# A two-unit loop body with a reordered slot, and transposes as two 64-row halves, in a software-pipelined attention and feed-forward kernel

## The chip, the cores and the metric

The kernel runs on one core of a Trainium2 chip. The core has five engines that run their own instruction streams and meet only in semaphores: TensorE (PE; its weight loads are shown apart as PEld), VectorE (DVE), ScalarE (ACT), GpSimd (POOL) and SyncE (SP, which starts the DMAs). The metric is the device time of one launch in microseconds (us); the kernel before takes 3991.84 us, the median of three runs (3988.70 to 3993.46). The profile is of one further execution, which took 3979.11 us.

## The reference

Batch 32, sequence 128, width 128, float32. First comes one cross-attention layer with residual, then a layer norm, then six layers of local attention and feed-forward, then the second residual. A "unit" below is one batch row in one of the six layers, so there are 6 x 32 = 192 units:

```python
for i in range(DEPTH):                                   # DEPTH = 6
    x = attn_layer(shift_tokens(x), Wqkv[i], q_scale[i], k_scale[i], Wo[i]) + x
    x = ffn_layer(shift_tokens(x), ln_g[i], ln_b[i], W1[i], b1[i], W2[i], b2[i]) + x
# attn_layer: q, k, v = split(x @ Wqkv) into 16 heads of 64
#   q = rotary(l2norm(q) * qs) * scale;  k = rotary(l2norm(k) * ks) / scale
#   softmax over windows of 32 queries and the 64 keys of this and the previous window
#   out = (softmax @ v) @ Wo
# ffn_layer: layer norm, a, gate = split(xn @ W1 + b1);  (a * gelu(gate)) @ W2 + b2
```

`shift_tokens` moves half of the channels by one token.

## The kernel before

After the cross-attention phase the kernel runs "slots". In slot n each engine executes its part of a fixed, hand-written list for several units at once: queries and keys of unit a = n are projected, unit m = n-1 is normalized, unit b = n-2 is transposed, scored and put through the softmax, unit c = n-3 is multiplied with its values, and unit d = n-4 gets output projection and feed-forward. Semaphore counts carry every dependence. Within a slot the engines do this:

- PE: `proj_qk(0)`, two groups of 4 transposes (L1089, queries), the token-shift matmuls of `zm` (L1119, L1120), `proj_qk(1)`, the transposes of the keys (L1089), `proj_qk(2)`, the transpose of the next input (L1134), `scores` (L1144, L1152), the transposes of the softmax P (L1167), the transpose of the normalized row (L1172), `proj_qk(3)`, the two W1 products (L1181, L1185), `proj_v(0)`, `attend` (L1103), `proj_v(1)`, the W2 product (L1201, "y2") and last the Wo product (L1210, "y"). The values of unit b are projected two slots after its queries, so the transposed input `zsT` has four buffers, and the loop body holds four slots.
- ACT copies what PE wrote from the PSUM banks: squares of the projections (L552), queries and keys (L561), P (L605), `zsT`, `znT` (L612); then a table load (L615), the fourth square, gelu (L623), a table load (L626), exp (L630), values (L568) and attention output `oT` (L574).
- DVE: `rotary(j)` (L814, a multiply into `ta` and one into `tb` for each of four banks), nine small operations `root(0)` to `root(8)` (L822 to L841) for 1/norm, the feed-forward residual chain `zm`, mean and variance, `zn` (L851 to L885), row maximum and subtraction (L896, L901), `hT` (L913), the row sums of P (L920), the sums of squares `ss` (L926), the reciprocal (L930) and `z_sb`, the unit's result (L935).
- POOL: `add(j)` (L436) joins `ta` and `tb`, `normalize(j)` (L445) multiplies by 1/norm, L478 multiplies P by the reciprocal; L452, L467 and L472 are small.
- SP copies values with a row offset (`shift_v`) and reloads the weights of the next layer.

The loop over slots is a `Fori` (the profile gives its register and branch instructions the line L244); 45 passes of four slots run in it, the first ten and the last eight slots are written out. The cross-attention phase has a loop of its own (L259 for its branch).

## Time and profile before

| | |
|---|---|
| median of 3 runs | 3991.84 us |
| profiled execution | 3979.11 us, span 3977.3 us |
| PE busy | 3528.5 us, 89%, 60708 matmul instructions and as many weight loads |
| DVE, ACT, POOL busy | 3481.0 us (88%), 2616.5 us (66%), 2522.5 us (63%) |
| mean granted TensorE clock | 0.965 of full |

A float32 product is shown as two matmul instructions with a weight load each, a transpose as one. Busy PE time is not PE at its peak, since matmuls are pipelined. The span splits into the cross-attention phase and start (about 0 to 400 us), the written-out first slots, the loop, and the written-out end (from 3842 us).

### The profile page before, as it was taken

The numbers are of one execution on the slowest core, as the hardware profiler recorded it, in microseconds if no ns is written. First come the engines' busy times: TensorE is split into PE (matmuls) and PEld (weight loads), VectorE is DVE, ScalarE is ACT, GpSimd is POOL, SyncE is SP. The second block draws the span as 40 slices with busy tenths as digits, with TensorE's granted clock in tenths as the row PEclk, the third lists the DMA queues.
The fourth block names the chain that finished last, engine by engine and source line by source line (L and its number), as shares of the span: only waits on it lengthen the run. The fifth ranks groups of instructions, "written<-read, shape, count | busy, mean of one in ns | idle before, by whom it ended". The sixth has DMA issues, their size and how long they took to land.

```text
span 3977.3 us, 158623 instructions
## 1 busy us (share of the span) xinstructions
PE 3528.5 (89%) x60708; PEld 2531.4 (64%) x60708; DVE 3481.0 (88%) x7219; ACT 2616.5 (66%) x4783; POOL 2522.5 (63%) x2671
## 2 busy tenths in 40 slices
PE   6887799998998989989989989989989889899997
PEld 3444476666666666666666666666666666666665
DVE  7888898998898988889989988889889889888895
ACT  3445676776676766667767676666667667666675
POOL 3334576766666766666667666666667667666673
PEclk9878899999999999999999999999999999999998
DMA  2000111112211112211111211112211112211112
GB/s 66 5 5 4 25 49 44 48 44 54 66 42 50 42 49 55 59 50 42 50 42 54 67 42 50 42 42 67 53 47 45 47 45 60 61 42 45 47 44 60
DMA packets 126086, 184.83 MB, mean 46 GB/s; under 512 B 26742, under 2 KB 49332, under 8 KB 124724
## 3 DMA queue, kind: packets, MB, share of 16 engines
q1 hardware_dynamic: 125492, 175.28, 17.2%
q8 instruction: 571, 9.36, 0.9%
q14 instruction: 23, 0.19, 0.0%
HBM read 21.32 MB, written 2.10 MB: 6 GB/s over the span
## 4 chain that ended last, share of the span: by engine, by line
PE 53%; ACT 21%; issue 20%; DVE 4%; ACTq 1%; POOL 0%; DMA 0%; DVEq 0%; SPq 0%; POOLq 0%
PE bank L1066 13%; PE bank L1210 10%; PE bank L1089 9%; PE bank L1152 6%; ACT L615 6%; ACT oT L574 4%; ACT gl L623 4%; PE bank L1167 4%; PE bank L972 2%; ACT znT L612 2%; ACT L626 2%; ACT vt L568 2%; PE bank L1144 2%; PE bank L1013 1%; PE bank L1120 1%
## 5 line engine op out<-in xcount | busy, mean ns | idle before, releaser
L436 POOL TENSOR_TENSOR qk<-ta,tb 128x512 f32<-128x512 f32 x768 | 971.6, 1275 | 513.3 <-DVE tb L814 513.3
L552 ACT ACTIVATE sq<-bank 128x512 f32<-128x512 f32 x768 | 459.3, 598 | 777.9 <-PE bank L1066 771.2
L1066 PE MATMUL bank<-wqkv,zsT 128*128 128x512 f32 x1536 | 831.1, 624 | 114.0 <-issue 104.9
L445 POOL TENSOR_TENSOR qk<-qk,rn 128x512 f32<-128x512 f32 x768 | 776.5, 1042 | 72.9 <-DVE rn L841 72.9
L814 DVE TENSOR_TENSOR ta<-bank,rot 128x512 f32<-128x512 f32 x768 | 529.4, 689 | 259.5 <-ACT sq L552 259.3
L478 POOL TENSOR_TENSOR P<-P,rowsum 128x512 f32<-128x512 f32 x384 | 393.6, 1044 | 498.9 <-DVE rowsum L930 498.9
L814 DVE TENSOR_TENSOR tb<-bank,rot 128x512 f32<-128x512 f32 x768 | 523.0, 681 | 0.0
L1089 PEld LDWEIGHTS bank<-cst,qk 128*128 128x128 f32 x3072 | 376.4, 146 | 214.4 <-issue 213.6
L1210 PE MATMUL bank<-wo,oT 128*128 128x128 f32 x3072 | 393.6, 281 | 130.3 <-ACT oT L574 130.2
L1210 PEld LDWEIGHTS bank<-wo,oT 128*128 128x128 f32 x3072 | 357.4, 191 | 167.1 <-ACT oT L574 128.5
L926 DVE TENSOR_REDUCE ss<-sq 128x32 f32<-128x2048 f32 x192 | 437.0, 2276 | 0.0
L1077 PE MATMUL bank<-wqkv,zsT 128*128 128x512 f32 x768 | 414.6, 622 | 10.8 <-DVE tb L814 4.2
L1089 PE MATMUL bank<-cst,qk 128*128 128x128 f32 x3072 | 415.0, 280 | 0.0
L605 ACT ACTIVATE PT<-bank 128x512 f32<-128x512 f32 x384 | 209.0, 595 | 305.4 <-PE bank L1167 305.4
L1103 PEld LDWEIGHTS bank<-PT,vs 64*64 64x64 f32 x18432 | 286.9, 135 | 145.7 <-issue 145.7
L1152 PE MATMUL bank<-kT,qT 64*32 64x64 f32 x24576 | 291.4, 224 | 41.1 <-issue 40.9
L1066 PEld LDWEIGHTS bank<-wqkv,zsT 128*128 128x128 f32 x1536 | 239.9, 197 | 132.0 <-issue 117.5
L1152 PEld LDWEIGHTS bank<-kT,qT 64*32 64x32 f32 x24576 | 281.3, 105 | 58.4 <-issue 48.1
L920 DVE TENSOR_REDUCE rowsum<-P 128x16 f32<-128x1024 f32 x192 | 234.2, 1220 | 93.1 <-ACT P L630 92.6
L1103 PE MATMUL bank<-PT,vs 64*64 64x32 f32 (+1 forms) x18432 | 308.1, 220 | 0.0
L1181 PEld LDWEIGHTS bank<-znT,w 128*128 128x128 f32 (+1 forms) x1152 | 138.6, 181 | 191.1 <-ACT znT L612 137.4
L411 POOL TENSOR_TENSOR qk<-qk,xmax 128x512 f32<-128x512 f32 x128 | 129.8, 1045 | 203.5 <-DVE xmax L715 203.5
(135 smaller groups left out, 6924.6 us busy)
## 6 DMA issues: line engine op xcount, KB each, us to landing
vs<-vt SPq DMA_DIRECT2D x1152, 128.0 KB, 2.4
wqkv<-L_ffn_Wqkv SPq DMA_DIRECT2D x6, 1024.0 KB, 4.9
wqkv<-L_ffn_Wqkv SPq DMA_DIRECT2D x6, 512.0 KB, 3.8
wo<-L_ffn_Wo SPq DMA_DIRECT2D x6, 512.0 KB, 4.2
z_sb<-x SPq DMA_DIRECT2D x4, 512.0 KB, 6.8
ctxb<-ctx SPq DMA_DIRECT2D x32, 64.0 KB, 1.7
out<-x_sb SPq DMA_DIRECT2D x8, 256.0 KB, 3.5
w<-L_ffn_W SPq DMA_DIRECT2D x6, 341.0 KB, 3.0
```

Of the source, the lines that this page charges most:

```text
L436: g.tensor_tensor(o, i0, i1, ALU.add).then_inc(s["g_add"], 1)
L445: g.tensor_tensor(q3, q3, r3, ALU.mult).then_inc(s["g_qk"], 1)
L478: g.tensor_tensor(pr, pr, rowsum[:, 1, 8 * j:8 * j + 8].unsqueeze(2).to_broadcast([128, 8, DH]), ALU.mult).then_inc(s["g_P"], 1)
L552: a_.activation(sq[:, 512 * j:512 * j + 512], bank[j % 2][:, :], ACT.Square)\
L814: ins = v_.tensor_tensor(t[:, 512 * j:512 * j + 512].rearrange("p (h d) -> p h d", d=DH), src, r.unsqueeze(1).to_broadcast([128, 8, DH]), ...
L926: v_.tensor_reduce(ss[:, pa, :], sq[:, :].rearrange("p (h d) -> p h d", d=DH), AX.X, ALU.add)\
L1066: t_.matmul(bank[j % 2][:, :], zsT[:, k % 4, :], wqkv[:, 512 * j:512 * j + 512], start=True, stop=True).then_inc(s["p_qk"], 1)
L1077: t_.matmul(bank[r][:, :], zsT[:, (k + 2) % 4, :], wv[:, :, r, :], start=True, stop=True)\
L1089: ins = t_.transpose(bank[4 + j % 2][:, 128 * p:128 * p + 128], qk[:, pb, 512 * j + 128 * p:512 * j + 128 * p + 128], ident)
L1103: ins = t_.matmul(bank[4 + r][64 * e:64 * e + 64, 128 * i + q0:128 * i + q0 + nq], vs[kr, pc, w, hc:hc + 64], PT[kr, 4 * e + i, q0:q0 + nq ...
L1152: ins = t_.matmul(SC[e][32 * w:32 * w + 32, 64 * p:64 * p + 64], qT2[dr, p, 32 * w:32 * w + 32], kT2[dr, p, k0:k0 + 64], start=False, stop ...
L1210: ins = t_.matmul(bank[7][:, 384:512], oT[:, p, :], wo[:, 2 * (p % 4) + p // 4, :], start=p == 0, stop=p == PAIRS - 1)
```

## The change

Five things are done together.

1. The loop body holds two slots (`LOOP0, UNROLL = 6, 2`). To allow it, the values of a unit are projected in the same slot as its queries (`proj_v` and `copy_v` go by a, not b), and `zsT` has two buffers.
2. PE: y2 (now of unit f = n-5) and y leave the slot's end and stand behind the first transposes of the next slot, ahead of `proj_qk(1)`. The transposes of P go ahead of `scores`, the transpose of the next input behind it.
3. Each full transpose (128 rows of tokens against a 128x128 identity) becomes two halves of 64 rows against a 64x64 identity, one into bank 4, one into bank 5. ACT's copies write 64-token stripes of all eight head pairs in place of four whole pairs.
4. DVE: root(1), root(3) to root(8) and the feed-forward chain change places, `ss` goes ahead of `rowsum`, and the write of `z_sb` goes behind rotary(0) of the next slot. POOL does normalize(0) and normalize(1) ahead of add(1). ACT copies P ahead of `zsT`.
5. SP's order at a layer's end follows the new lags, and there is one more slot at the end.

```diff
-        zsT = sb("zsT", [128, 4, S])
+        zsT = sb("zsT", [128, 2, S])
-        LOOP0, UNROLL = 8, 4
-        LOOP1 = UNITS - 4
+        LOOP0, UNROLL = 6, 2
+        LOOP1 = UNITS - 2
...
-                def transpose_qk(j):
-
-                    wait(pe, "g_qk", count(4, b, j + 1))
-                    if j < 2:
-                        edge(pe, n, "a_tr", count(4, b - 1, j + 3))
-                        wait(pe, "a_AV", count(2, c - 1, j + 1))
+                def transpose_rows(src, sem_name):
+
+                    for p in range(PAIRS):
+                        for t in range(2):
+                            tok = slice(64 * t, 64 * t + 64)
+                            ins = t_.transpose(bank[4 + t][:, 64 * p:64 * p + 64], src[tok, 128 * p:128 * p + 128],
+                                               ident[tok, tok])
+                            if p == PAIRS - 1:
+                                ins.then_inc(s[sem_name], 1)
+
+                def transpose_qk(i):
+
+                    wait(pe, "g_qk", count(4, b, 2 * i + 2))
+                    if i == 0:
+                        edge(pe, n, "a_tr", count(4, b - 1, 4))
+                        wait(pe, "a_AV", count(2, c - 1, 2))
                     else:
-                        wait(pe, "a_tr", count(4, b, j - 1))
-                    for p in range(4):
-                        ins = t_.transpose(bank[4 + j % 2][:, 128 * p:128 * p + 128],
-                                           qk[:, pb, 512 * j + 128 * p:512 * j + 128 * p + 128], ident)
-                    ins.then_inc(s["p_tr"], 1)
+                        wait(pe, "a_tr", count(4, b, 2))
+                    pe.nop(nofuse=True)
+                    transpose_rows(qk[:, pb, 1024 * i:1024 * i + 1024], "p_tr")
...
+                if c_on:
+
+                    wait(pe, "g_P", count(2, c, 2))
+                    wait(pe, "a_tr", count(4, b, 4))
+                    edge(pe, n, "a_AV", count(2, c - 1, 2))
+                    pe.nop(nofuse=True)
+                    transpose_rows(P[:, pc, :], "p_PT")
                 if b_on:
                     scores()
...
                 if m_on:
                     root(0)
+                    root(1)
+                if a_on:
+                    rotary(0)
+                if m_on:
+                    root(2)
+                if f_on:
+
+                    wait(dve, "p_y2", count(1, f, 1))
+                    wait(dve, "g_zmb", count(1, f, 1))
+                    v_.tensor_tensor(z_sb[:, cols(f)], bank[6][:, 384:512], zmb[:, pf, :], ALU.add)\
+                        .then_inc(s["z_ready"], 1)
+                if m_on:
+                    root(3)
+                    root(4)
```

On PE, inside the loop, from the end of one slot to the keys of the next. Before (L1077 values, L1103 attend, L1201 y2, L1210 y, L1066 queries and keys, L1089 transposes, L1119 and L1120 zm):

```order
L1103 MATMUL bank<-PT,vs 64x32 x8
L222 REGISTER_ALU
L1077 MATMUL bank<-wqkv,zsT 128x512
L222 ISA
L1201 MATMUL bank<-w,hT 128x128 x3
L1210 MATMUL bank<-wo,oT 128x128 x8
L222 ISA x2
L222 REGISTER_ALU
L1066 MATMUL bank<-wqkv,zsT 128x512
L1089 MATMUL bank<-cst,qk 128x128 x8
L222 REGISTER_ALU
L1119 MATMUL bank<-zm,cst 128x64
```

And of the change (L1081 values, L1071 queries and keys, L1152 y2, L1161 y, L1171 and L1172 zm):

```order
L1081 MATMUL bank<-wqkv,zsT 128x512
L222 ISA x2
L222 REGISTER_ALU
L1071 MATMUL bank<-wqkv,zsT 128x512
L222 ISA
L1089 MATMUL bank<-cst,qk 128x64 x16
L222 ISA
L1152 MATMUL bank<-w,hT 128x128 x3
L222 ISA
L1161 MATMUL bank<-wo,oT 128x128 x8
L1071 MATMUL bank<-wqkv,zsT 128x512
L222 REGISTER_ALU
```

y2 and y moved from ahead of the slot's first projection to behind its first transposes, and the transposes are 16 halves in place of 8 whole ones.

On DVE, the seam between two slots. Before (L920 rowsum, L926 ss, L930 reciprocal, L935 z_sb, L822 root(0), L851 zm, L827 root(1), L814 rotary(0)):

```order
L920 TENSOR_REDUCE rowsum<-P 128x16
L926 TENSOR_REDUCE ss<-sq 128x32
L930 RECIPROCAL rowsum<-rowsum 128x16
L935 TENSOR_TENSOR z_sb<-bank,zmb 128x128
L222 REGISTER_ALU
L822 TENSOR_SCALAR ss<-ss 128x32
L851 REGISTER_ALU
L851 ISA
L851 TENSOR_TENSOR zm<-bank,z_sb 128x128
L222 ISA x2
L827 TENSOR_SCALAR rn<-ss 128x32
```

And of the change, from root(1) (L834) to zm (L872), with rotary(0) at L821, root(2) L836, z_sb L862, root(3) L838, root(4) L840:

```order
L834 TENSOR_SCALAR rn<-ss 128x32
L222 ISA x2
L821 TENSOR_TENSOR ta<-bank,rot 128x512
L821 TENSOR_TENSOR tb<-bank,rot 128x512
L222 REGISTER_ALU
L836 SCALAR_TENSOR_TENSOR nr<-ss,rn 128x32
L862 TENSOR_TENSOR z_sb<-bank,zmb 128x128
L222 REGISTER_ALU
L838 TENSOR_TENSOR nr<-nr,rn 128x32
L222 REGISTER_ALU
L840 SCALAR_TENSOR_TENSOR rn<-nr,rn 128x32
L872 REGISTER_ALU
```

zm stood ahead of rotary(0) and now stands behind it, with z_sb and root(2) to root(4) between them.

## Rows read from the trace of the kernel before

**Rows 1.** The page: share of the chain that ended last, by engine.

```profile
PE 53%; ACT 21%; issue 20%; DVE 4%; ACTq 1%; POOL 0%; DMA 0%; DVEq 0%; SPq 0%; POOLq 0%
```

**Rows 2.** Instructions of line L244: engine, operation, count: min/median/max ns, first and last start.

```profile
L244 DVEq COMPARE_BRANCH  x45: 50/56/74, 610.7 to 3842.4; - x45
L244 PEldq COMPARE_BRANCH  x45: 76/3787/4122, 610.9 to 3842.4; - x45
```

**Rows 3.** The same of line L259, the cross-attention loop.

```profile
L259 PEldq COMPARE_BRANCH  x13: 83/215/249, 79.7 to 370.1; - x13
```

**Rows 4.** Timeline behind a branch, at 2007 us; in brackets the idle time before.

```profile
2007.68 2.07 PE L1066 MATMUL bank<-wqkv,zsT 128*128 128x512 f32 x2 [2.30 <-issue]
```

**Rows 5.** Timeline of DVE, 1900 to 2120 us: start, us, engine, line, instruction.

```profile
1951.19 0.23 DVE L935 TENSOR_TENSOR z_sb<-bank,zmb 128x128 f32 x1
...
1968.93 0.23 DVE L935 TENSOR_TENSOR z_sb<-bank,zmb 128x128 f32 x1
...
1986.08 0.23 DVE L935 TENSOR_TENSOR z_sb<-bank,zmb 128x128 f32 x1
```

**Rows 6.** Timeline of DVE and POOL in an undisturbed slot, 2021 to 2031 us.

```profile
2021.68 0.85 DVE L913 SCALAR_TENSOR_TENSOR hT<-bank,b1c,gl 128x128 f32<-128x128 f32 x3
...
2023.26 1.22 DVE L920 TENSOR_REDUCE rowsum<-P 128x16 f32<-128x1024 f32 x1 [0.72 <-ACT P L630]
...
2024.39 2.27 DVE L926 TENSOR_REDUCE ss<-sq 128x32 f32<-128x2048 f32 x1
...
2026.59 0.24 DVE L930 RECIPROCAL rowsum<-rowsum 128x16 f32<-128x16 f32 x1
...
2026.91 2.05 POOL L478 TENSOR_TENSOR P<-P,rowsum 128x512 f32<-128x512 f32 x2 [2.69 <-DVE rowsum L930]
...
2027.23 0.76 DVE L827 TENSOR_SCALAR rn<-ss 128x32 int32<-128x32 int32 x1
...
2028.47 0.69 DVE L814 TENSOR_TENSOR ta<-bank,rot 128x512 f32<-128x512 f32 x1 [0.47 <-ACT sq L552]
...
2029.84 1.28 POOL L436 TENSOR_TENSOR qk<-ta,tb 128x512 f32<-128x512 f32 x1 [0.88 <-DVE tb L814]
...
2029.98 1.18 DVE L831 TENSOR_TENSOR nr<-nr,rn 128x32 f32<-128x32 f32 x1
```

**Rows 7.** Timeline of PE and ACT in the same slot, 2028 to 2038 us.

```profile
2028.36 0.33 PE L1119 MATMUL bank<-zm,cst 128*128 128x64 f32 x2
...
2028.53 0.39 PE L1120 MATMUL bank<-zm,cst 128*128 128x64 f32 x2
...
2028.76 1.08 PE L1066 MATMUL bank<-wqkv,zsT 128*128 128x512 f32 x2
...
2030.36 1.08 ACT L561 ACTIVATE kT<-bank 128x512 f32<-128x512 f32 x2
...
2031.61 0.41 PE L1144 MATMUL bank<-maskb,selb 64*32 64x512 bf16 x8
...
2033.22 1.09 PE L1167 MATMUL bank<-cst,P 128*128 128x128 f32 x8
...
2034.88 0.46 ACT L612 ACTIVATE znT<-bank,gb 128x128 f32<-128x128 f32 x1
...
2035.37 1.28 ACT L615 ACT_TABLE_LOAD   x1
...
2036.83 1.02 PE L1077 MATMUL bank<-wqkv,zsT 128*128 128x512 f32 x2
...
2037.79 1.60 PE L1103 MATMUL bank<-PT,vs 64*64 64x64 f32 x96
```

**Rows 8.** Groups by line and shape: count, busy us, mean ns of one, idle before.

```profile
L1089 PEld LDWEIGHTS bank<-cst,qk 128*128 128x128 f32 x3072 | 376.4, 146 | 214.4 <-issue 213.6 <-POOL qk L445 0.5
L1210 PEld LDWEIGHTS bank<-wo,oT 128*128 128x128 f32 x3072 | 357.4, 191 | 167.1 <-ACT oT L574 128.5 <-issue 38.7
L1103 PEld LDWEIGHTS bank<-PT,vs 64*64 64x64 f32 x18432 | 286.9, 135 | 145.7 <-issue 145.7
```

More of the change, by code:

```diff
@@ L246, in slots @@
                     body(i * UNROLL + (LOOP0 + k), LOOP0 + k)
-            for n in range(LOOP1, UNITS + 4):
+            for n in range(LOOP1, UNITS + 5):
                 body(n, n)
@@ L344, in _ @@
             for layer in range(DEPTH):
-                first = B * layer + 2
+                start, end = B * layer, B * layer + B
                 if layer == 0:
-                    shift_v(0, 0)
-                    shift_v(1, 1)
+                    for u in range(3):
+                        shift_v(u, u % 2)
                 with sp.Fori(0, (B - 6) // 2) as i:
                     for k in range(2):
-                        shift_v(i * 2 + (first + k), k)
-                shift_v(B * layer + B - 4, 0)
+                        shift_v(i * 2 + (start + 3 + k), (3 + k) % 2)
+                shift_v(end - 3, 1)
                 if layer + 1 < DEPTH:
                     load_qk(layer + 1)
-                for k in range(3):
-                    shift_v(B * layer + B - 3 + k, (1 + k) % 2)
+                shift_v(end - 2, 0)
                 if layer + 1 < DEPTH:
                     load_v(layer + 1)
-                    shift_v(B * layer + B, 0)
+                shift_v(end - 1, 1)
+                if layer + 1 < DEPTH:
+                    shift_v(end, 0)
+                    shift_v(end + 1, 1)
                     load_o(layer + 1)
-                    shift_v(B * layer + B + 1, 1)
+                    shift_v(end + 2, 0)
                     load_ffn(layer + 1)
@@ L456, in slot @@
                 if m_on:
-                    for j in range(4):
-                        normalize(j)
+                    normalize(2)
+                    normalize(3)
                 if a_on:
@@ L853, in slot @@
                 if m_on:
-                    root(1)
-                if a_on:
-                    rotary(0)
-                if m_on:
-                    root(2)
+                    root(5)
+                    root(6)
                 if d_on:
@@ L863, in slot @@
                 if m_on:
-                    root(3)
+                    root(7)
                 if d_on:
@@ L870, in slot @@
                 if m_on:
-                    root(4)
+                    root(8)
                 if d_on:
@@ L911, in slot @@
                     wait(dve, "p_y2", count(1, d - 1, 1))
[L912 to L914 removed]
+                    for j, (_, w) in enumerate(FCH):
+                        ins = v_.scalar_tensor_tensor(hT[0:w, j, :], bank[6][0:w, 128 * j:128 * j + 128],
+                                                      b1c[0:w, j:j + 1], gl[0:w, j, :], ALU.add, ALU.mult)
                     ins.then_inc(s["d_h"], 1)
[L916 to L921 removed]
                 if a_on:
@@ L928, in slot @@
                 if b_on:
+                    wait(dve, "a_exp", count(1, b, 1))
+                    wait(dve, "d_rec", count(1, b - 1, 1))
+                    v_.tensor_reduce(rowsum[:, 0, :], P[:, pb, :].rearrange("p (h t) -> p h t", t=DH), AX.X, ALU.add)\
+                        .then_inc(s["d_sum"], 1)
                     wait(dve, "d_sum", count(1, b, 1))
+                    wait(dve, "g_P", count(2, b - 1, 2))
                     v_.reciprocal(rowsum[:, 1, :], rowsum[:, 0, :]).then_inc(s["d_rec"], 1)
-                if d_on:
-                    wait(dve, "p_y2", count(1, d, 1))
-                    wait(dve, "g_zmb", count(1, d, 1))
-                    v_.tensor_tensor(z_sb[:, cols(d)], bank[6][:, 384:512], zmb[:, pd, :], ALU.add)\
-                        .then_inc(s["z_ready"], 1)
             slots(dve, slot)
@@ L1050, in slot @@
                 d, d_on = part(n, 4)
+                f, f_on = part(n, 5)
                 pb, pc, pd = k % 2, (k - 3) % 2, k % 2
@@ L1155, in scores @@
                     ins.then_inc(s["p_S"], 1)
+                if a_on:
+                    proj_qk(0)
+                if b_on:
+                    transpose_qk(0)
+                if f_on:
+                    wait(pe, "d_h", count(1, f, 1))
+                    wait(pe, "l_w2", 48 * layer_of(f) + 48)
+                    for j, (_, m) in enumerate(FCH):
+                        ins = t_.matmul(bank[6][:, 384:512], hT[0:m, j, :], w2[0:m, j, :], start=j == 0, stop=j == 2)
+                    ins.then_inc(s["p_y2"], 1)
@@ new lines, in slot @@
+                if d_on:
+                    wait(pe, "a_AV", count(2, d, 2))
+                    wait(pe, "l_wo", 16 * layer_of(d) + 16)
+                    edge(pe, n, "a_gelu", count(1, d - 1, 1))
+                    edge(pe, n, "a_zs", count(2, zu - 1, 2))
+                    for p in range(PAIRS):
+                        ins = t_.matmul(bank[7][:, 384:512], oT[:, p, :], wo[:, 2 * (p % 4) + p // 4, :], start=p == 0,
+                                        stop=p == PAIRS - 1)
+                    ins.then_inc(s["p_y"], 1)
@@ new lines, in slot @@
+                if a_on:
+                    proj_qk(1)
+                if d_on:
+                    wait(pe, "d_zm", count(1, d, 1))
+                    wait(pe, "z_ready", (count(1, f, 1) if isinstance(f, int) else d) + B)
+                    t_.matmul(bank[6][:, 0:64], ident, zm[:, pd, 0:64], start=True, stop=True)
+                    t_.matmul(bank[6][:, 64:128], shift, zm[:, pd, 64:128], start=True, stop=True)\
+                        .then_inc(s["p_zsh"], 1)
+                if b_on:
+                    transpose_qk(1)
```

127 lines of the change are left out of this document (37 added, 90 removed).

## The prediction

> **What bounds the kernel now.** I read the page first, then the rows of the loop's branch, then the DVE timeline over some slots, then one slot on all engines. The chain that ended last lies 53% on PE, 21% on ACT and 20% on "issue" [rows 1]: PE and ACT hand each other the slot, and a fifth is time in which nothing visible is waited for. The branch rows say where much of that comes from. The loop's branch costs DVE 56 ns, but PE 3787 ns at the median, in each of 45 passes [rows 2]; in the small cross-attention loop the same PE instruction took 215 ns [rows 3]. Behind it PE's first projection stands 2.30 us on "issue" [rows 4].
>
> The starts of z_sb give the slot's length: 17.74 and 17.15 us for two neighbours without a branch [rows 5]. From DVE's first to its last branch 44 passes take 3842.4 - 610.7 = 3231.7 us [rows 2], 73.45 us a pass, 18.36 a slot. Four slots of 17.15 would be 68.60, so a pass loses 4.85 us to the branch and the pauses around it, 218 us over 45 passes.
>
> So there are two questions: does the branch's stall go, and how long is an undisturbed slot in the new order. The second decides as much as the first: 0.1 us a slot is 19 us in all.
>
> **The loop body.** Two-slot body, 92 passes in place of 45 (184 slots in place of 180). By the table PE has 60708 matmuls and as many weight loads for 192 units, 632 a unit (a little high, since it counts the cross-attention too). Transposes as halves add 24 matmuls and 24 loads a unit, so the body falls from about 2530 instructions to about 2 x 680 = 1360. If PE's branch is then cheap, as for the small body [rows 3], the stall is gone. If not, it comes 92 times. The rows only bracket this: cheap for a small body, dear at 2530. I take "cheap", at three chances in four, since DVE's branch shows that going back is not dear in itself [rows 2] and since the body is nearly halved.
>
> The Trainium skill, page "Runtime: NRT & Kernel Launch", section "Instruction fetch mechanics", gives PE room for 2048 instructions, refilled in blocks of 256, and says in the same section that a taken branch whose target is outside the current two-block window must fetch it first. By the first figure 1360 fits and 2530 does not, which the two branch rows agree with; by the second the stall stays. That second reading is rival C below.
>
> **The new slot.** I work the ring of work that has to close, from rotary(0) of one slot to rotary(0) of the next, with time 0 at the start of its first multiply.
>
> DVE up to zm. Today root(3) (L831) starts at 1.51 and takes 1.18 instead of some 0.2, and ends just as POOL's add(0) ends: 2031.16 against 2031.12 [rows 6]. It waits for POOL. With z_sb in the place of the variance step it meets the same add, so root(3) ends at 2.69. root(4) and zm (each like the small rows of 0.24) end at about 3.13. New is that PE's token-shift matmuls now wait for this zm, and behind them in PE's queue stand the key transposes, the third projection, P's transposes and the scores. PE starts them at 3.23; they take 2028.76 - 2028.36 = 0.40 [rows 7], to 3.63.
>
> Half transposes. A group of 8 whole ones takes about 0.87 (L1167 with its tail 1.09, [rows 7]; 0.109 each). One group becomes 16 halves. Nearest row: attend, 96 products on 64x64 pieces of the array in 1.60, less a tail of about 0.22, 14.5 ns each [rows 7]. A weight load of 64 columns lasts 135 ns there, one of 128 columns 191 [rows 8], so 64 columns cost 56 ns and the rest is latency; at 14.5 ns each the four pieces must load side by side. A whole transpose's load lasts 146 ns [rows 8], 45 less than the ordinary one, so it costs 112 - 45 = 67; two pieces side by side give 0.034 us a half. I take 0.035, 0.56 a group. Ends: 0.0118 each, the pace of the scores (136 products in 1.61, [rows 7]), 0.19 a group; 0.109 each, if a half costs as much as a whole one, 1.74.
>
> The Trainium skill, page "TensorEngine Tiling (Array Packing)", section "Key Properties", says that tiles load and multiply in parallel but that changing the tiling mode drains the engine. The first half is what attend shows; the second half agrees with the charge below.
>
> A change of shape costs 0.10: attend starts at 2037.79, 0.06 ahead of the modelled end of the projection before it (2036.83 + 1.02), while a product of the same shape starts 0.16 ahead of that end (2028.76 against 2028.53 + 0.39) [rows 7].
>
> Keys: 3.63 + 0.10 + 0.56 = 4.29. ACT's copies of both halves need both banks finished, start at 4.53 and take 1.09 [rows 7], to 5.62. P's transposes use the same two banks, so they wait for them (new; before, they stood behind the scores): 5.77, to 6.33. Scores: 0.10 and 2033.22 - 2031.61 = 1.61 [rows 7], to 8.04. Then the input transpose, ACT's two short copies (0.35 after, then 0.55) and znT at 8.94, the table load at 9.43 (0.49 on, [rows 7]), the fourth square at 10.72, ended at 11.32, rotary(3) at 11.50.
>
> DVE to the seam: rotary(3) 1.21; hT 0.77; ss 2.20; rowsum 1.13 (starts differ by 2026.59 - 2024.39 and 2024.39 - 2023.26); from the reciprocal to the end of root(1) 2027.99 - 2026.59 = 1.40, less the 0.08 by which DVE starts ahead, 1.32 [rows 6]. root(1) today waits for the first of POOL's two multiplies, which starts 0.32 after the reciprocal; in the new order root(1) comes at about 0.36 and meets it again. Sum: 11.50 + 6.63 = 18.13 us.
>
> What is hidden: root(7), which today also waits for an add, stands where POOL is idle, but only on DVE, which then waits for the scores. The stall at y for oT goes, yet the ring now passes from zm through both transposes and the fourth square. PE and ACT alone (through exp and the value copy to proj_qk(0)) I estimate from the same terms at 16.9, so DVE's seam comes last by about 1.2. SP's reordered copies and reloads have a slot more than before; I cost them at nothing; were that cover gone, a weight load's some 5 us at each of five layer edges, 25 us.
>
> Sum against the profiled 3979.1: 180 loop slots at 18.13 + 0.02 for the branch in place of 18.36, -38; about 12 full written-out slots at +0.98, +12; the extra slot's y2 and z_sb, some +2. That is 3955. The median of the runs shown lies 12.7 above the profiled execution, so 3968.
>
> **Rivals.**
> A. The same mechanism, my slot right to 0.3: 3968, own range 3890 to 4050.
> B. The seam is free: root(1) slips in front of POOL's multiply (the margin is 0.04 us), or the halves run at the scores' pace. Without the root(1) wait the ring is 1.03 shorter, 17.1: 3968 - 1.03 x 192 = 3770. At 0.0118 a half the two groups in the ring save 0.74, giving 3826. Both together meet the PE and ACT ring at about 16.9 less the same savings, some 3700. For it: the margin; against it: POOL's start is released by the reciprocal itself, root(1) by a chain of two.
> C. The change doesn't remove the code stall. PE has about 1.1 us of slack before the zm matmuls, and part of 3.8 overlaps the end of the last group, so a branch costs about 1.3 in the ring, 92 x 1.3 = 120; the pauses inside a pass (17.15 + 17.15 + 17.74 against three even slots: 0.3 a slot) add 57. 3968 + 177 = 4145, slower. If nothing overlaps, 92 x 3.6 = 331 and 57: 4356.
> D. Halves hardly run side by side: from 0.067 each, one load after the other, where a group is 1.07, the two in the ring cost +1.02, 4164; at 0.109 it is +2.36 and 4421. Against it: attend [rows 7]. It decides from 0.04 each on.
>
> **How the numbers follow.** A 0.42, B 0.27, C 0.20, D 0.11; B's margin of 0.04 us is small against hops that I read to 0.02 to 0.05, C is the quarter left open above, less what DVE's cheap branch takes off, and attend's row speaks against D. A change under 0.2%, 8 us, can't be told from none by a measurement of this kernel. Within A I give faster 0.22, within 0.2% 0.08, slower 0.12, as its centre lies 24 us below 3992 and its error is twice that and more. With B faster, C and D slower: faster 0.49, same 0.08, slower 0.43. The range takes in A whole, the upper two thirds of B and most of C's near value: 3760 to 4170; the likeliest case alone has 3890 to 4050.
>
> **What would show it.** PE's branch at some 0.2 us in 92 passes for the loop; the start of a group of 16 halves to the next instruction, 0.56; the starts of z_sb every 18.1 us; root(1) at 0.7 and root(3) at 1.2 us as today; DVE idle before the first row maximum (about 0.7) and before rotary(3) (0.8), PE idle in front of the token-shift matmuls (about 1.1). I am wrong if the slot is below 17.5 with a cheap branch (then a wait that I put into the ring isn't there), or if the branch still takes microseconds.

## The result, and the profile after

| | before | after |
|---|---|---|
| median of 4 runs each | 3992.65 us | 4206.54 us (4199.48 to 4212.37) |
| ratio | | 1.0516, 95% interval 1.0458 to 1.0574 |
| profiled span | 3977.3 us | 4197.7 us |
| mean granted TensorE clock | 0.965 | 0.948 |

The change makes the kernel 5.2% slower. The forecast was 3968 us, and 4206 lies outside its range.

The page after: engines' busy time, the instruction queue's transfers, and the share of each engine in the chain that ended last.

```profile
PE 3553.4 (85%) x65316; PEld 2356.9 (56%) x65316; DVE 3503.9 (83%) x7219; ACT 2659.1 (63%) x4785; POOL 2515.8 (60%) x2671
...
q8 instruction: 30, 0.49, 0.0%
...
DVE 37%; PE 30%; issue 16%; ACT 12%; DVEq 3%; ACTq 0%; DMA 0%; POOL 0%; SPq 0%; POOLq 0%
```

In [rows 1] the chain ran 53% over PE and 4% over DVE; now DVE has 37%. The bound has moved to DVE and the work around it.

The loop's branch, as in [rows 2] (min/median/max ns, then first and last start):

```profile
L244 PEldq COMPARE_BRANCH  x92: 76/208/242, 543.3 to 4092.1; - x92
```

PE's 3787 ns are now 208, so the code stall is gone as forecast. The 91 passes between the first and the last branch take (4092.1 - 543.3) / 91 = 39.00 us each, 19.50 a slot, against 18.36 before. The next view shows where. Its stretches run from the start of one reciprocal to the next (start and end, length, PE busy with its count, granted clock, DMA share, GB/s):

```profile
2049.38:2067.68 18.30, 16.04 (x333) 1.00 0.16 41
2067.68:2087.36 19.68, 16.44 (x335) 1.00 0.17 42
...
2105.66:2126.52 20.86, 17.78 (x334) 0.92 0.16 40
...
2144.81:2167.06 22.25, 19.18 (x335) 0.85 0.15 37
```

Two slots form a pass. The one that starts inside the body takes 18.30 us every time. The one that starts at the loop's edge takes 19.68 at full clock, and up to 22.25 where the granted clock falls below 1.00; its mean over the loop is 20.72. I call the first "plain slot" and the second "edge slot". So there are two losses a pass: 19.68 - 18.30 = 1.38 us that need no fall of the clock, and 20.72 - 19.68 = 1.04 us more that come with it.

**The edge.** DVE's timeline (start us, us, line, operation; idle time in brackets), first over a plain slot's start, then over an edge slot's start, with POOL:

```profile
2125.18 1.20 DVE L937 TENSOR_REDUCE rowsum<-P 128x16 f32<-128x1024 f32 x1
2126.52 0.25 DVE L941 RECIPROCAL rowsum<-rowsum 128x16 f32<-128x16 f32 x1
2126.69 0.12 DVE L829 TENSOR_SCALAR ss<-ss 128x32 f32<-128x32 f32 x1
2126.86 2.04 POOL L483 TENSOR_TENSOR P<-P,rowsum 128x512 f32<-128x512 f32 x2 [2.56 <-DVE rowsum L941]
...
2126.95 0.99 DVE L834 TENSOR_SCALAR rn<-ss 128x32 int32<-128x32 int32 x1
2127.85 0.68 DVE L821 TENSOR_TENSOR ta<-bank,rot 128x512 f32<-128x512 f32 x1
```

```profile
2105.66 0.25 DVE L941 RECIPROCAL rowsum<-rowsum 128x16 f32<-128x16 f32 x1
...
2105.99 2.04 POOL L483 TENSOR_TENSOR P<-P,rowsum 128x512 f32<-128x512 f32 x2 [2.46 <-DVE rowsum L941]
2106.14 0.93 DVE L829 TENSOR_SCALAR ss<-ss 128x32 f32<-128x32 f32 x1 [0.23 <-issue]
...
2107.22 0.85 DVE L834 TENSOR_SCALAR rn<-ss 128x32 int32<-128x32 int32 x1
2107.99 0.68 DVE L821 TENSOR_TENSOR ta<-bank,rot 128x512 f32<-128x512 f32 x1
```

In the plain slot root(0) (L829) starts 0.17 us after the reciprocal and is done in 0.12, ahead of POOL. Only root(1) (L834) meets POOL's first multiply of P and lasts 0.99. At the edge the branch stands behind the reciprocal (2105.74). root(0) loses 0.23 us, and starts after POOL's multiply has begun at 2105.99. It now lasts until the first of POOL's two multiplies is over (0.93), and root(1) until the second is (0.85). From the reciprocal to rotary(0) (L821) it is 1.33 us in one case and 2.33 in the other. So 1.00 of the 1.38 us arises here. The other 0.38 builds up in small steps on several engines over the rest of the slot; root(3), for one, lasts 1.27 us for 1.17. No run takes these steps apart.

Before, the order was rowsum, ss, reciprocal [rows 6], and DVE's sequencer went through its branch while the 2.2 us of `ss` ran: 0.30 us after the start of `ss`, at the median over the passes. The change puts `ss` first. A branch that nobody saw is now in the open.

**The clock.** PE's timeline of the same two slots, the plain one first:

```profile
2131.27 0.43 PE L1171 MATMUL bank<-zm,cst 128*128 128x64 f32 x2 [1.43 <-DVE zm L872]
...
2131.86 0.71 PE L1089 MATMUL bank<-cst,qk 64*128 64x64 f32 x16
2132.50 1.13 PE L1071 MATMUL bank<-wqkv,zsT 128*128 128x512 f32 x2
```

```profile
2111.51 0.43 PE L1171 MATMUL bank<-zm,cst 128*128 128x64 f32 x2 [2.33 <-DVE zm L872]
...
2112.09 0.71 PE L1089 MATMUL bank<-cst,qk 64*128 64x64 f32 x16
2112.73 1.73 PE L1071 MATMUL bank<-wqkv,zsT 128*128 128x512 f32 x2
2114.39 1.12 PE L1089 MATMUL bank<-cst,P 64*128 64x64 f32 x16
```

PE waits for DVE's `zm` 1.43 us in a plain slot and 2.33 in an edge slot. Behind the longer wait its work slows down: the projection L1071 takes 1.73 us for 1.13, the P transposes 1.12 for the 0.71 of the key transposes just ahead of the fall. TensorE's clock records know two levels, full (2.4 GHz) and half (1.2 GHz). Within the loop they give the lower one for 96 us in all before, and for 266 us after; "low" below means this, counted from the start of the loop to PE's last branch.

These rows also settle the halves: 16 of them take 2132.50 - 2131.86 = 0.64 us.

### The profile page after: what moved, and what is told of

It reads as the page before. It is cut to its first block, busy times and chain, and to the rows that moved or that the text cites. A ratio compares the mean times of both kernels' runs of the same rounds, so it can differ in the third digit from the quotient of the medians.

```text
span 4197.7 us, 169870 instructions
## 1 busy us (share of the span) xinstructions
PE 3553.4 (85%) x65316; PEld 2356.9 (56%) x65316; DVE 3503.9 (83%) x7219; ACT 2659.1 (63%) x4785; POOL 2515.8 (60%) x2671
## 4 chain that ended last, share of the span: by engine, by line
DVE 37%; PE 30%; issue 16%; ACT 12%; DVEq 3%; ACTq 0%; DMA 0%; POOL 0%; SPq 0%; POOLq 0%
DVE ss L931 7%; PE bank L1089 7%; PE bank L1138 6%; PE bank L1071 6%; ACT L621 6%; DVE nr L838 6%; DVE rowsum L937 5%; DVE tb L821 4%; DVE hT L924 4%; DVE ta L821 2%; DVE ss L829 2%; ACT gl L629 2%; PE bank L977 2%; PE bank L1171 2%; DVEq L222 2%
## 5 line engine op out<-in xcount | busy, mean ns | idle before, releaser
L1071 PE MATMUL bank<-wqkv,zsT 128*128 128x512 f32 x1536 | 879.1, 656 | 96.3 <-ACT vt L573 90.7
L447 POOL TENSOR_TENSOR qk<-qk,rn 128x512 f32<-128x512 f32 x768 | 786.4, 1047 | 3.8 <-DVE rn L848 3.8
L821 DVE TENSOR_TENSOR ta<-bank,rot 128x512 f32<-128x512 f32 x768 | 528.1, 688 | 241.3 <-ACT sq L557 226.3
L566 ACT ACTIVATE kT<-bank 128x512 f32<-128x512 f32 x384 | 208.5, 595 | 513.7 <-PE bank L1089 513.7
L821 DVE TENSOR_TENSOR tb<-bank,rot 128x512 f32<-128x512 f32 x768 | 521.2, 679 | 0.0
L1081 PE MATMUL bank<-wqkv,zsT 128*128 128x512 f32 x768 | 414.5, 622 | 5.0 <-DVE tb L821 5.0
L1071 PEld LDWEIGHTS bank<-wqkv,zsT 128*128 128x128 f32 x1536 | 240.1, 197 | 274.3 <-ACT vt L573 241.8
L454 POOL TENSOR_TENSOR rstd<-ve,half_neg 128x1 f32<-128x1 f32 x192 | 105.7, 550 | 465.7 <-DVE ve L892 465.7
L1171 PE MATMUL bank<-zm,cst 128*128 128x64 f32 x384 | 85.1, 305 | 351.4 <-DVE zm L872 351.4
L1161 PE MATMUL bank<-wo,oT 128*128 128x128 f32 x3072 | 376.4, 276 | 1.6 <-ACT oT L579 1.5
L1161 PEld LDWEIGHTS bank<-wo,oT 128*128 128x128 f32 x3072 | 360.0, 192 | 2.0 <-ACT oT L579 2.0
L907 DVE TENSOR_REDUCE rowmax<-bank 128x8 f32<-128x512 f32 x384 | 247.3, 686 | 131.4 <-PE bank L1138 131.4
L1171 PEld LDWEIGHTS bank<-zm,cst 128*128 128x128 f32 x384 | 58.9, 193 | 506.9 <-issue 497.5
L1089 PEld LDWEIGHTS bank<-cst,qk 64*128 64x128 f32 x6144 | 236.6, 147 | 166.5 <-issue 152.2
L1138 PEld LDWEIGHTS bank<-kT,qT 64*32 64x32 f32 x24576 | 293.4, 110 | 20.9 <-issue 12.8
```

The source lines that it names most:

```text
L447: g.tensor_tensor(q3, q3, r3, ALU.mult).then_inc(s["g_qk"], 1)
L821: ins = v_.tensor_tensor(t[:, 512 * j:512 * j + 512].rearrange("p (h d) -> p h d", d=DH), src, r.unsqueeze(1).to_broadcast([128, 8, DH]), ...
L1071: t_.matmul(bank[j % 2][:, :], zsT[:, k % 2, :], wqkv[:, 512 * j:512 * j + 512], start=True, stop=True).then_inc(s["p_qk"], 1)
L1081: t_.matmul(bank[r][:, :], zsT[:, k % 2, :], wv[:, :, r, :], start=True, stop=True)\
L1089: ins = t_.transpose(bank[4 + t][:, 64 * p:64 * p + 64], src[tok, 128 * p:128 * p + 128], ident[tok, tok])
L1138: ins = t_.matmul(SC[e][32 * w:32 * w + 32, 64 * p:64 * p + 64], qT2[dr, p, 32 * w:32 * w + 32], kT2[dr, p, k0:k0 + 64], start=False, stop ...
```

## The experiments

All times are medians; ratios are to runs of the kernel before on the same chip. That kernel took 3980.8 to 4019.1 us on the chips used, so a difference in microseconds between kernels run on different chips can be off by up to 1%; the readings below rest on the slots in the traces. "Pair" is the length of a plain and of an edge slot, as means over the loop. "Seam" in the expectations is the edge. The diffs are shortened: `ss(a)`, `zm(d)` and the like stand for all lines of that step.

| kernel | us | ratio, 95% interval | pair, us |
|---|---|---|---|
| changed | 4206.5 | 1.0516 (1.0458 to 1.0574) | 18.30 + 20.72 |
| changed, filler on PE | 4110.6 | 1.0227 (1.0191 to 1.0262) | 18.31 + 19.68 |
| changed, zm early | 3817.0 | 0.9504 (0.9471 to 0.9537) | 16.78 + 18.06 |
| changed, sums in the old order | 4439.9 | 1.1043 (1.1001 to 1.1086) | 20.62 + 20.85 |
| changed, zm early and old sums | 3903.5 | 0.9719 (0.9686 to 0.9753) | 17.82 + 17.91 |
| changed, root(0) ahead | 4030.7 | 1.0071 (1.0045 to 1.0097) | 17.95 + 19.21 |
| changed, zm early, root(0) and root(1) ahead | 3724.1 | 0.9306 (0.9269 to 0.9342) | 16.68 + 17.17 |
| the same with whole transposes | 3767.1 | 0.9408 (0.9371 to 0.9445) | 16.88 + 17.48 |
| changed, whole transposes | 4188.9 | 1.0536 (1.0496 to 1.0576) | 18.45 + 20.44 |
| changed, body of four slots | 4365.4 | 1.0979 (1.0937 to 1.1021) | - |
| before, body of two slots | 3824.7 | 0.9620 (0.9584 to 0.9656) | 17.34 + 17.64 |
| before, body of two, halves | 3861.3 | 0.9708 (0.9671 to 0.9744) | 17.50 + 17.81 |
| before, halves alone | 4125.2 | 1.0326 (1.0259 to 1.0394) | - |

### Is it the clock? Dummy work in PE's wait

```diff
                 if d_on:
+                    wait(pe, "d_sub", count(2, b - 1, 2))
+                    for _ in range(12):
+                        t_.transpose(SC[0][:, 0:128], ident, ident)
                     wait(pe, "d_zm", count(1, d, 1))
```

> The changed kernel with twelve transposes of the identity added on TensorE just ahead of its wait for zm, into a scores bank that is free there; nothing reads them, and they take about 1.3 us of a wait of 1.43 or 2.33 us. Theory of the clock: TensorE no longer stands idle for 2.3 us, the clock does not fall, the projection behind it goes from 1.73 back to 1.13 us and the transposes of P, scores and keys with it; 1.0 us a pair, 4206 - 95 = about 4110 us, low-clock time from 438 towards 250 us. Theory of the seam alone, or halves or code: extra instructions gain nothing, 4200 to 4230 us.

4110.6 us. PE does 2304 transposes more, and the kernel is 96 us faster than the changed one by the medians (2.9% of the kernel before by the ratios; the two ran on different chips). The stretches of the filler kernel:

```profile
2067.85:2087.53 19.68, 17.75 (x347) 1.00 0.17 42
2087.53:2105.84 18.31, 17.34 (x345) 1.00 0.16 41
```

and its PE behind the wait, in an edge slot:

```profile
2109.20 1.47 PE L1169 MATMUL bank<-cst 128*128 128x128 f32 x12
2111.70 0.43 PE L1173 MATMUL bank<-zm,cst 128*128 128x64 f32 x2 [1.02 <-DVE zm L872]
...
2112.92 1.13 PE L1071 MATMUL bank<-wqkv,zsT 128*128 128x512 f32 x2
```

Every edge slot now takes the 19.68 us that the changed kernel had where its clock held, and every plain slot is as it was. The wait of 2.33 us has become 1.02, and the projection takes 1.13 us. The clock is never low in the loop. So the clock is worth 1.04 us x 92 = 96 us, and the edge's 1.38 us stays: they are two causes.

### Is it the edge? Sums in the old order, and root(0) ahead of the branch

```diff
-                ss(a)          # sums first: rowsum(b), ss(a), reciprocal(b)
                 rowsum(b)
+                ss(a)
                 reciprocal(b)
```

> The changed kernel with the sums at the slot's end in the order of the kernel before: rowsum, ss, reciprocal instead of ss, rowsum, reciprocal, so that VectorE's sequencer reaches the loop's branch while ss still runs. Theory of the seam: from reciprocal to rotary(0) both slots of a pair then take the same, about 1.3 us (now 2.3 and 1.3), and the two slots come out within 0.4 us of each other. The price is the wait of rowsum for exp ahead of ss, up to 1.0 us a slot, so the time may stay: 4206 - 100 + (0 to 180) = 4106 to 4290 us. Theory of the clock alone: the longer slot stays longer by 2 us or more. Rival, halves or code: no change in either.

4439.9 us, a miss in size. The edge did go, as the theory says: 20.62 and 20.85, 0.23 us apart in place of 2.42. But all slots are long. rowsum now waits for exp ahead of `ss`, 1.07 us in the first row, and the clock is low in every slot (0.92 in the second view), for 676 us in the loop against 266:

```profile
2088.30 1.22 DVE L931 TENSOR_REDUCE rowsum<-P 128x16 f32<-128x1024 f32 x1 [1.07 <-ACT P L636]
```

```profile
2050.24:2071.03 20.79, 17.68 (x335) 0.92 0.15 38
```

I had priced the wait and not what goes with it at PE: PE waits about 2.3 us for `zm` in both slots here, and the clock fell at every one of these waits. The run with both moves below, where the clock stays up, has the price of the wait alone.

The second test leaves the order of the sums and moves one small instruction:

```diff
                     v_.tensor_reduce(rowsum ...)
+                if a_on:
+                    root(0)       # of unit a; taken away from the start of the next slot
+                if b_on:
                     v_.reciprocal(...)
```

> The changed kernel with root(0) of the next slot moved ahead of reciprocal, behind rowsum, in the slot where its ss is made; nothing else. Theory of the seam: the loop's branch costs 0.2 us itself, and 1.0 to 1.1 us only because root(0) then comes after the pool's multiply of P has begun and waits for it, so that root(1) waits for the second multiply. With root(0) ahead of the reciprocal only root(1) stands behind the branch and waits for the first multiply, as in the other slot: pair from 18.30 + 20.72 to 18.3 + 18.3 to 18.5, and as TensorE's wait for zm shrinks by the same microsecond its clock stays up too: 4206 - 126 - 96 + (0 to 20) = about 3990 to 4010 us. Rival, the branch itself (or what every engine does at the loop's edge) costs the 1.37 us: the seam slot stays 1.3 us or more longer, 4080 to 4206 us.

4030.7 us, 176 less than the changed kernel; 196 to 216 were expected. The edge slot's median is 18.68, 0.73 above the plain slot's 17.95 where 1.38 was. DVE of this kernel at the edge, then in a plain slot:

```profile
2106.63 0.16 DVE L829 TENSOR_SCALAR ss<-ss 128x32 f32<-128x32 f32 x1
2106.74 0.25 DVE L943 RECIPROCAL rowsum<-rowsum 128x16 f32<-128x16 f32 x1
2107.37 0.79 DVE L834 TENSOR_SCALAR rn<-ss 128x32 int32<-128x32 int32 x1 [0.37 <-issue]
2108.07 0.68 DVE L821 TENSOR_TENSOR ta<-bank,rot 128x512 f32<-128x512 f32 x1
...
2125.42 0.25 DVE L943 RECIPROCAL rowsum<-rowsum 128x16 f32<-128x16 f32 x1
2125.64 0.18 DVE L834 TENSOR_SCALAR rn<-ss 128x32 int32<-128x32 int32 x1
2125.97 0.69 DVE L821 TENSOR_TENSOR ta<-bank,rot 128x512 f32<-128x512 f32 x1
```

One thing I had not foreseen: in the plain slot root(1) is now the instruction that gets in ahead of POOL, and lasts 0.18 us. At the edge it starts 0.63 us after the reciprocal in place of 0.22, meets the multiply and lasts 0.79. So at the seam about 0.4 us is the branch itself (0.63 for 0.22), and the rest is the multiplies that DVE misses. The clock's falls did not go altogether (low for 137 us in the loop, with PE's wait for zm at 1.3 us in the edge slots): that part of the forecast was too good.

The Trainium skill, page "SBUF — State Buffer", section "SBUF: two separate sides", says that VectorE and GpSimd share one pair of ports under an exclusive lock, taken by whichever starts first and held for a whole instruction, and that only some VectorE instructions need it. The traces agree: root(0) takes 0.12 or 0.93 us by its place before or behind POOL's start, while rotary(0), which reads PSUM, takes 0.68 with POOL's second multiply beside it (plain slot) and with that multiply all but over (edge).

### The wait for zm

```diff
                 z_sb(f)
+                zm(d)
                 if m_on:
                     root(3)
                     root(4)
-                zm(d)
```

> The changed kernel with one move: VectorE's add of zm stands ahead of the two q/k norm steps root(3) and root(4), not behind them; root(3) takes 1.2 us there because it waits for the pool's add. Theory of the clock: TensorE waits 2.33 us for zm in one slot of each pair and 1.43 in the other, its clock falls only behind the longer wait, and the fall costs about 1.0 us a pair. The waits should become 1.1 and 0.2 us, the falls of the clock vanish from the loop (low-clock time from 438 us towards 250 us), and the path to zm is shorter as well: about 1.0 us a pair for the clock and up to 1.3 a slot for the path, 4206 - 95 - (0 to 240) = 3870 to 4110 us. Theory of the seam alone (VectorE's branch in the open, 1.0 to 1.4 us a pair): the pair still has one slot about 1.3 us longer than the other, and the rest of the gain is that of the path. Rival, the halves or the code loading cost the time: the time stays within 20 us of 4206.

3817.0 us, 390 less than the changed kernel (by the slots, 4.18 x 92 = 385), and 53 below the lowest time that I had allowed. In the changed kernel root(3) (L838) ends only with POOL's add, and `zm` (L872) comes behind it:

```profile
2109.44 1.26 POOL L438 TENSOR_TENSOR qk<-ta,tb 128x512 f32<-128x512 f32 x1 [1.41 <-DVE tb L821]
2109.49 1.27 DVE L838 TENSOR_TENSOR nr<-nr,rn 128x32 f32<-128x32 f32 x1
...
2111.08 0.29 DVE L872 TENSOR_TENSOR zm<-bank,z_sb 128x128 f32<-128x128 f32 x1
```

root(3) lasts about 1.2 us in every slot, and PE's queue stood behind `zm`. With the move, PE's wait in an edge slot is

```profile
2112.37 0.43 PE L1171 MATMUL bank<-zm,cst 128*128 128x64 f32 x2 [0.72 <-DVE zm L869]
```

in place of 2.33. The plain slot falls by 18.30 - 16.78 = 1.52 us: `zm` was on the path in every slot. The clock is never low in the loop, in place of 266 us. The edge is still there, 18.06 - 16.78 = 1.28, as two separate causes require.

Both moves together:

> Both moves at once: zm ahead of root(3) and root(4), and rowsum, ss, reciprocal at the end. If seam and clock are two causes, the pair's two slots come out alike and the clock stays up: time below each of the single moves if the wait for exp is short, 3900 to 4100 us. If the two are one cause, it is no better than zm ahead alone.

3903.5 us, slots 17.82 and 17.91. The edge is gone, and without the falls of the clock the old order of the sums costs 1.04 us in the plain slot, the wait for exp that had been priced. In both slots together that is more than the edge: 17.82 + 17.91 against 16.78 + 18.06, and 86 us slower than zm early alone. The time alone is the outcome that I had set down for one cause only. It came about although there are two, because the wait for exp is not short. The slots do come out alike, as two causes require, but with `zm` early the clock was up already; what tells the two apart is the filler.

### Parts of the change by themselves

The loop alone, in the slot order of before. Values are projected with their own unit's queries, `zsT` has two buffers, and SP's order is that of the changed kernel:

```diff
-        zsT = sb("zsT", [128, 4, S])
+        zsT = sb("zsT", [128, 2, S])
-        LOOP0, UNROLL = 8, 4
-        LOOP1 = UNITS - 4
+        LOOP0, UNROLL = 6, 2
+        LOOP1 = UNITS - 2
-                if b_on:
+                if a_on:
                     proj_v(0)
```

> The kernel before, slot order and whole transposes as they were, with only the loop's body cut to two slots; for it v is projected with q and k of the same unit, so that two zsT buffers are enough. Theory that the loop alone gains and the new order gives it back: the 3.8 us branch per four slots becomes 0.2 us per two, and VectorE's branch stays beneath ss; slots as before within the body, 17.1 to 17.3 us, 3992 - 200 = about 3790 us (3760 to 3850). Rival: each turn of a two-slot loop costs 2 us or more in any order: then 3970 to 4000 us.

3824.7 us, 3.8% faster than before. Its branch and its DVE at the edge:

```profile
L244 PEldq COMPARE_BRANCH  x92: 76/208/237, 537.2 to 3720.2; - x92
```

```profile
2109.49 1.22 DVE L922 TENSOR_REDUCE rowsum<-P 128x16 f32<-128x1024 f32 x1 [0.45 <-ACT P L632]
2110.62 2.28 DVE L928 TENSOR_REDUCE ss<-sq 128x32 f32<-128x2048 f32 x1
2112.82 0.24 DVE L932 RECIPROCAL rowsum<-rowsum 128x16 f32<-128x16 f32 x1
```

DVE's branch comes at 2110.92, 0.3 us into the 2.28 us of `ss`. The edge costs 0.30 us a pass, not 1.38. So the loop gives its gain in an order that hides DVE's branch, and a two-slot loop as such is not the cause.

With the halves as well (transposes of two banks at a time as 64-row halves, as in the change):

> As the one before, with the transposes of queries, keys and softmax as two 64-row halves. Group of sixteen halves 0.64 us against 0.87 for eight whole ones; against that a group waits for the later of two pool adds. Theory: TensorE is not the bound at these places, so within 0.3 us a slot of the two-slot body alone: 3760 to 3850 us. Rival, the halves cost through their wait for both adds or through the clock: 0.5 us a slot or more, 3880 us and above.

3861.3 us, 0.16 us a slot and 37 us more, between the two outcomes set down. The halves cost a little there.

The changed kernel with whole transposes:

```diff
-                    for p in range(PAIRS):
-                        for t in range(2):
-                            ...  # 64-row halves, bank[4 + t]
+                    for j in range(2):
+                        for p in range(4):
+                            q = 4 * j + p
+                            ins = t_.transpose(bank[4 + j][:, 128 * p:128 * p + 128],
+                                               src[:, 128 * q:128 * q + 128], ident)
```

> The changed kernel with whole 128-row transposes, two groups of four, in place of the halves; loop and slot order as changed. Theory (seam and clock from the new order): the halves are not the cause, three groups of eight take 0.87 instead of 0.64 us, 0 to 0.7 us a slot more: 4206 to 4340 us. Rival, the halves cost the time: below 4150 us.

4188.9 us, 18 less than with halves, by runs of two chips whose kernel before differs by 0.3%. By ratio, 1.0536 against 1.0516, they are the same. That is below the range set down and above what the rival would give. The plain slot is 0.15 us longer (18.45), the clock is low for 119 us in place of 266, and the two about cancel. So the halves are not the cause of the slowdown as a whole, though with them the clock falls more often.

The changed kernel with four slots in the body (`UNROLL = 4`):

> The changed kernel with a body of four slots instead of two. Theory: the branch of TensorE takes about 3.8 us again, once per four slots, and one slot in four instead of one in two carries the seam and the clock's fall: + 0.95 us a slot for code, less 2.4/4 = 0.6 us a slot: + 0.35 a slot, 4206 + 65 = 4270 us (4200 to 4330). If code loading were free at any body size the time would be 4206 - 110 = 4095 us.

4365.4 us, 95 above the forecast and outside its range. The branch is dear again, and behind it the first projection waits 6.71 us, with another pause of 1.61 in the middle of the scores:

```profile
L244 PEldq COMPARE_BRANCH  x46: 83/3718/4009, 583.5 to 4255.7; - x46
```

```profile
2111.44 0.34 PE L1138 MATMUL bank<-kT,qT 64*32 64x64 f32 x13 [1.61 <-issue]
...
2142.90 2.07 PE L1071 MATMUL bank<-wqkv,zsT 128*128 128x512 f32 x2 [6.71 <-issue]
```

The four slots of a pass take 17.98, 25.51, 18.44 and 19.69 us. Between two branches PE has about 2740 instructions here and 1380 in the changed kernel, and the instruction queue moves 620 packets for 30. With nothing else changed, the body's size decides whether code is loaded.

The halves alone, in the slot order and the four-slot body of before:

> The kernel before with one part of the change alone: the transposes of queries, keys and softmax as two 64-row halves, in the old slot order and the four-slot body. In the two-slot body the halves cost 37 us (3861 against 3825), 0.2 us a slot, though a group of them is 0.2 us shorter, because the first group now waits for the second add of the pair. If that is the cause it shows here too: 4003 + 20 to 40 = 4020 to 4040 us. If the halves were slow in themselves (issue, change of shape), the group of sixteen would take longer than 0.7 us. The larger number of instructions in the body (about 2650 in place of 2530) may lengthen the branch of 3.8 us: up to 0.3 us more, 14 us.

4125.2 us, 138 more where 20 to 40 were expected. It is a miss, and an instructive one. Between two branches PE has 2742 instructions in place of 2557. The branch is hardly longer (3864 ns at the median), but pauses inside the body come oftener. This is one of them, in the middle of a group of P transposes:

```profile
2067.51 0.59 PE L1086 MATMUL bank<-cst,P 64*128 64x64 f32 x12 [1.75 <-issue]
```

Pauses of over 1.5 us within the loop that PE spends on "issue", those at the branches left out, number 50 and take 92 us in this kernel, against 16 and 32 us before, and the instruction queue moves 618 packets for 571. The clock is low for 236 us in the loop in place of 96. In the two-slot body, where the queue moves 30 packets in all, the same halves cost 37 us. So in the four-slot body they seem to cost mainly as code. The remaining 100 us were not separated. An estimate: the pauses take 60 us more, and at the changed kernel's rate (96 us for 266 us of low clock) the further 140 us of low clock would cost some 50.

### The version that beats both

`zm` early, and root(0) and root(1) of the next slot ahead of the reciprocal:

```diff
                     v_.tensor_reduce(rowsum ...)
+                if a_on:
+                    root(0)
+                    root(1)
+                if b_on:
                     v_.reciprocal(...)
```

> zm ahead of root(3) and root(4), and root(0) and root(1) of the next slot ahead of reciprocal. From 3817 us with slots of 16.78 and 18.06: the seam's 1.28 us a pair goes (-118 us: 3700), and root(1) no longer waits 0.85 us for the pool's multiply, which is worth up to 0.85 us a slot (-156 us: 3545) if VectorE is still the bound there and nothing if TensorE is. 3545 to 3720 us, most likely about 3650. If the seam were not this wait: 3800 us or more.

3724.1 us, 6.9% faster than before and 11.5% faster than the changed kernel; the range set down ended at 3720. DVE at the edge:

```profile
2094.48 0.17 DVE L829 TENSOR_SCALAR ss<-ss 128x32 f32<-128x32 f32 x1
2094.68 0.18 DVE L834 TENSOR_SCALAR rn<-ss 128x32 int32<-128x32 int32 x1
2094.77 0.25 DVE L942 RECIPROCAL rowsum<-rowsum 128x16 f32<-128x16 f32 x1
2095.55 0.69 DVE L821 TENSOR_TENSOR ta<-bank,rot 128x512 f32<-128x512 f32 x1 [0.53 <-issue]
```

Neither root meets POOL. From the reciprocal to rotary(0) it is 0.78 us at the edge, with the branch in it, against 2.33. Of the 118 us that the edge was worth (1.28 - 0.49) x 92 = 73 came, since 0.49 us of it are left. The further 156 us, due if DVE had stayed the bound, did not come but for 0.10 a slot, 18 us: the plain slot went only from 16.78 to 16.68. PE and ACT are the bound now: by its page the chain that ended last lies 57% on PE, 24% on ACT and 4% on DVE, where the changed kernel has 37% on DVE. A piece of it runs from ACT's exp over its value copy to PE's projection:

```profile
2108.16 0.15 ACT P L636
...
2109.12 0.59 ACT vt L573
...
2109.75 1.12 PE bank L1072 x2
```

The same with whole transposes:

> As the one before, with whole 128-row transposes. The halves were worth nothing in the changed order (4189 whole, 4206 halves) and cost 37 us in the order of before (3825 whole, 3861 halves). If TensorE is now the bound, the 0.23 us that a group of halves saves show at last: 0 to 100 us slower than the halves; if the gain is not in TensorE's time, the same or up to 20 us faster.

3767.1 us, 43 more by the medians. Here the halves do gain, 0.26 us a slot, once PE is in the ring that sets the time.

## Why the prediction was wrong

**The code stall: right.** Predicted 0.2 us in 92 passes, measured 0.208. The loop by itself gives 156 us where I said 218. The difference is in the slots: I took 17.15 us as what remains without the stall, and the two-slot kernel has 17.34 and 17.64, (17.49 - 17.15) x 184 = 63 us. The Trainium skill, page "Runtime: NRT & Kernel Launch", section "Instruction fetch mechanics", gives PE room for 2048 instructions. With that the traces agree: 1290 and 1380 instructions between branches are cheap, 2557 and more are not. Its other statement there, that a taken branch must fetch its target when it lies outside the two-block window, would make 1380 dear too, and the measurement is against it.

**The halves: right within 0.08 us a group.** Predicted were 0.035 us each and 0.56 a group; 0.64, 0.040 each, was measured from the start of the first to the start of the next instruction, in both kinds of slot. Rival D started at 0.067 each and is refuted, by the whole transposes too.

**The new slot: right for one slot in two.** The ring came out at 18.13; the plain slot has 18.30. root(1) met POOL's multiply and lasted 0.99, root(3) lasted 1.17 (1.27 in an edge slot) for 1.2, the row maximum waited 0.57 for 0.7. PE's idle time before the token-shift matmuls was to be about 1.1, and was 1.43.

**The edge: the step that failed.** "180 loop slots at 18.13 + 0.02 for the branch" charged the branch its own length. That is 0.04 us a pass. The instruction's own length is not what is paid: what counts is what the branch runs beneath, and what starts late behind it. I had the order of the sums before me in [rows 6] and knew that rowsum and `ss` change places, but checked only PE's side of the branch. In a plain slot root(0) starts 0.17 us after the reciprocal, at the edge 0.48, and POOL's multiply 0.33 after it, between the two. Price: 1.38 us a pass, 127 us in place of 4. Rival B had noticed such a race for root(1), and I looked only for the side on which it is won.

**The clock: not in the sum at all.** I took every duration from rows at full clock, and found PE's new wait harmless because PE was not the bound. In 69 of 91 edge slots the clock fell behind that wait, and the slowed work (projection, P transposes, scores) is in the ring. Price: 96 us, shown by the filler.

**Sum.** Against the two-slot loop with halves in the old order (3861), the changed order costs (18.30 - 17.50) x 184 = 147 us in plain length; (1.38 - 0.31) x 92 = 98 at the edge; 1.04 x 92 = 96 by the clock. That is 341 of the 345 us measured. From before: -156 (loop), +37 (halves), +345 (order) = +226, against +214; the 12 us between them are the difference of the kernel before on the two chips (3980.8 and 3992.7). Against the forecast the plain slots are (18.30 - 18.13) x 184 = 31 us longer, the edge adds 127 - 4 = 123 and the clock 96, together 250, where the forecast was missed by 4206 - 3968 = 238. The recorded mechanism for "slower", rival C, gave 4145, but for a stall that was not there; its neighbourhood to the result is chance. (Its pause term of 0.3 us a slot is 0.2 by its own three slots, (17.15 + 17.15 + 17.74) / 3 - 17.15.)

The direction of the 147 us was in my own numbers: undisturbed slots of 17.15 before [rows 5] against 18.13 in the new ring. They were weighed as equal to the 218 us of the loop, and that was about right for the sum; it left no room for a second loss.

## What to carry to other kernels

When a loop's order changes, look at each engine's last and first instructions around the branch: put a long instruction that waits for nothing late between the last wait and the branch, and keep short VectorE instructions that wait out a running GpSimd instruction (0.12 us became 0.93 here) ahead of what starts GpSimd. Where an engine's queue waits for a small result, compute that result ahead of anything that waits for a third engine; here one such move was worth some 390 us, the clock's share among them. And price a new wait of TensorE not only by who stands behind it, but by the clock at which they then run.

## What the runs showed of the hardware that I had not expected

- 12 useless transposes a slot made the kernel 96 us faster: PE kept the full clock with a wait of 1.02 us. In the changed kernel's loop the fall came at 69 of the 91 waits of 2.3 us at the edge, and at none of the 92 of 1.4 us. But with root(0) ahead it came at 40 of 91 waits of 1.3 us, with whole transposes at 35 of 91 of 2.2 us, and in the body of four slots at 6 of 45 of 1.4 us. So the length of this wait alone does not decide; what else does is open.
- A branch of 56 ns on VectorE delayed the next instruction by 0.31 us (root(0) of the changed kernel), 0.41 and 0.45 (the two kernels with roots ahead), and with a missed turn at GpSimd made rotary(0) 1.00 us late and the slot 1.38 us longer.
- Of two short VectorE instructions behind GpSimd's start, each waits out one GpSimd instruction: root(0) 0.93 us instead of 0.12, root(1) 0.85 instead of 0.18.
- A body of 2557 PE instructions or more pays for its code in several places: 3.8 us at the branch, and pauses of mostly 1.6 to 2.2 us in the middle of a group of transposes or scores, on which no wait is shown; 185 instructions more brought 34 more of these in the loop.
